# Expert results scattered to token order, context attention by halves, and slot experts with maxima found early and a split final product

## What is computed

```python
x = x + latent_attention(ctx, layernorm(x))        # 16 heads of 64; stage A
x = x + moe_top1(layernorm(x))                     # 8 experts, gelu, 1 choice; stage B
x = x + context_attention(layernorm(x), ctx)       # 16 heads of 16, 77 keys; stage C
x = x + (x_n + moe_sinkhorn(x_n))                  # 8 experts, 2 choices, gates; stage D
x = x + context_attention(layernorm(x), ctx)       # stage E
h = x_n + self_attention(rms(x_n)); x = x + h + moe_top2(rms(h))   # stage F
x = x + align(ctx, layernorm(x))                   # dynamic time warping; stage G
# stage H, slot experts: b batch, m token, n expert (64), p slot (32), d width
logits = einsum('bmd,dnp->bmnp', x_n, phi)
dispatch = softmax(logits, axis=0)                 # over the two batches
combine = softmax(logits over (n, p), axis=-1)
slots = einsum('bmd,bmnp->bnpd', x_n, dispatch)
y = einsum('bnpd,nde->bnpe', slots, W) + b
x = x + einsum('bnpd,bmnp->bmd', y, combine)
```

## Time and profile before

| | |
|---|---|
| three runs | 3989.61, 3993.71, 4001.67 us |
| profiled execution | 3996.7 us, its span 3994.9 us |
| granted clock of TensorE, mean | 0.872 |
| busy, share of the span | TensorE 75%, VectorE 53%, ScalarE 37%, GpSimd 25% |
| A, latent attention | 1200.0 us, TensorE busy 1075.7 |
| B, experts, one choice | 200.6 us, TensorE 102.6 |
| C and E, context attention with norms | 192.7 and 193.0 us, TensorE 148.9 and 151.0 |
| D, experts, sinkhorn, two choices | 424.7 us, TensorE 266.1 |
| F, self-attention, then experts, two choices | 624.0 and 415.0 us, TensorE 537.9 and 264.3 |
| G, alignment | 278.0 us, TensorE 40.0 |
| H, slot experts: first pass, second, final product | 254.3, 96.0, 116.6 us |

### The profile page before, as it was taken

The page is one execution under the profiler, slowest core; times in us unless marked ns, Lnnn a source line. Parts: engine busy times, 40 slices in busy tenths (PEclk is TensorE's granted clock), DMA queues, the critical chain, the costliest instruction groups (busy, mean ns, idle before and its releaser), DMA issues. The chain is left out here.

```text
span 3994.9 us, 40974 instructions
## 1 busy us (share of the span) xinstructions
PE 3001.8 (75%) x14054; PEld 1774.0 (44%) x14054; DVE 2109.9 (53%) x3706; ACT 1486.7 (37%) x2035; POOL 994.6 (25%) x586
## 2 busy tenths in 40 slices
PE   3999999999984568369658599999639940069879
PEld 1555555555534534259635233333339920034354
DVE  4655555555522345347536378788237737831270
ACT  3344444444442233336323245555426510022240
POOL 1346565555542202121213100000130040001100
PEclk7899999999996779579879789999769965579999
DMA  2000000000002400156300000000036420000150
GB/s 90 5 6 1 5 5 5 0 5 5 2 0 90 132 11 0 36 187 213 122 25 0 11 3 2 4 4 2 2 142 223 160 54 10 4 21 32 47 185 21
DMA packets 81429, 187.26 MB, mean 47 GB/s; under 512 B 19011, under 2 KB 55491, under 8 KB 73216
## 3 DMA queue, kind: packets, MB, share of 16 engines
q0 software_dynamic: 16464, 103.18, 7.7%
q1 hardware_dynamic: 61856, 76.11, 6.1%
q10 hardware_dynamic: 2960, 6.03, 0.4%
HBM read 145.65 MB, written 39.38 MB: 46 GB/s over the span
## 5 line engine op out<-in xcount | busy, mean ns | idle before, releaser
L602 POOL TENSOR_TENSOR A_key_sums<-A_key_sums,A_probs 128x1024 f32<-128x1024 f32 (+1 forms) x224 | 526.7, 2370 | 228.5 <-ACT A_probs L495 228.5
L495 ACT ACTIVATE A_probs<-A_banks 128x512 f32<-128x512 f32 (+1 forms) x576 | 329.0, 597 | 384.9 <-PE A_banks L415 382.7
L545 DVE TENSOR_REDUCE A_part_max<-A_banks 128x1 f32<-128x367 f32 x768 | 353.9, 530 | 157.1 <-PE A_banks L336 155.6
L1750 DVE TENSOR_REDUCE F_part_max<-F_banks 128x1 f32<-128x512 f32 x512 | 324.9, 683 | 56.8 <-PE F_banks L1603 54.0
L1696 ACT ACTIVATE F_probs<-F_banks 128x1024 f32<-128x1024 f32 x256 | 248.0, 1022 | 233.6 <-PE F_banks L1649 233.5
L364 PE MATMUL A_banks<-A_probs,A_v_tok 128*64 128x512 f32 x1152 | 278.7, 605 | 0.0
L413 PE MATMUL A_banks<-A_q_one,A_k_one 128*128 128x512 f32 (+1 forms) x576 | 255.6, 444 | 26.2 <-ACT A_probs L495 23.1
L336 PE MATMUL A_banks<-A_k_one,A_q_one 128*128 128x368 f32 x768 | 230.2, 383 | 6.8 <-ACT A_v_tok L475 6.4
L415 PE MATMUL A_banks<-A_q_two,A_k_two 128*128 128x512 f32 (+1 forms) x576 | 227.2, 394 | 0.0
L167 POOL TENSOR_SCALAR F_r<-F_r,F_ln_w 128x512 f32<-128x512 f32 x16 | 28.8, 1812 | 656.7 <-DVE F_r L132 656.7
L336 PEld LDWEIGHTS A_banks<-A_k_one,A_q_one 128*128 128x128 f32 x768 | 147.4, 192 | 94.7 <-DVE A_part_max L545 58.5
(11 more groups left out here) (537 smaller groups left out, 6262.2 us busy)
## 6 DMA issues: line engine op xcount, KB each, us to landing
H_w<-in_H_w SPq DMA_DIRECT2D x11, 1024.0 KB, 4.8
moe_in<-A_zeros ACTq DMA_DIRECT2D x1, 5888.0 KB, 17.3
D_tile_in<-moe_in SPq DMA_DIRECT2D x23, 256.0 KB, 5.3
moe_out<-D_z SPq DMA_DIRECT2D x23, 256.0 KB, 5.0
F_tile_in<-moe_in SPq DMA_DIRECT2D x23, 256.0 KB, 5.3
moe_out<-F_z SPq DMA_DIRECT2D x23, 256.0 KB, 4.8
H_phi<-in_H_w SPq DMA_DIRECT2D x5, 1024.0 KB, 4.9
B_tile_in<-moe_in SPq DMA_DIRECT2D x15, 256.0 KB, 3.0
```

Source lines behind the costliest of these rows:

```text
L495: act.activation(probs[0:kw, j, kt % RING, blk * BLK:(blk + 1) * BLK], ps[0:kw, half % 3, :], ACT.Exp, scale=1.0 / 8.0).then_inc(s["exp_re ...
L545: dve.tensor_reduce(part_max[:, i // 3, i % 3:i % 3 + 1], ps[:, MAX_BANKS[i % 3], 0:PIECE], AX.X, ALU.max).then_inc(s["piece_max"], 1)
L602: pool.tensor_tensor(key_sums[0:kw, j, :], before, probs[0:kw, j, kt % RING, :], ALU.add).then_inc(s["summed"], 1)
L1750: op = dve.tensor_reduce(part_max[:, maximum_at(hd, qt), kb:kb + 1], bank, AX.X, ALU.max)
```

## The change

The words of the change name an alignment in wave order; the alignment's code is the same in both kernels. What differs:

- **Scratch tensors.** Each expert layer has its own `moe_in` and `moe_out` in DRAM. `moe_in` has one more column (B) or five more (D, F) in each row. B's is zeroed at the start from ScalarE's queue, D's and F's from SyncE's within the latent attention.
- **Routing in the rows.** The added columns say for each row to which token it belongs, which expert was its first choice, and the gates. They take seven more small steps of VectorE before the rows are sent (one with one choice) and two more small loads.
- **Scattered results.** Per slot, VectorE works out from the loaded rows where each result goes (`find_rows`, four small steps, one with one choice) and multiplies the result by its gate where it copied it (L1093 for L1033). GpSimd scatters it with two indirect DMAs per slot to `moe_out`, which is now in token order by choice, with room behind for unused rows. In the tail SyncE loads blocks of 512 KB, TensorE adds the two choices by products with the identity, VectorE adds to x. The gathers and L1066, L1067 are gone.
- **Context attention by halves.** Maximum and difference run on two halves of 616, each with its own count; the scores of a half wait for the difference of that half only. The last block's four outputs use four banks and do not wait for each other.
- **Slot experts.** The maxima are found in the first pass, 1,024 numbers in each of the 32 steps, and one small one at its end. The second pass takes groups 12 to 15 first, whose slots are in SBUF, with the first group's weights loaded at the end of the first pass. The final product is a block of its own: its two factors are split into halves by ScalarE and VectorE, and TensorE does three single passes for each product.

The diff, cut:

```diff
-            sp.wait_ge(slots_zeroed, 16)
+            zero_rows(sp, t["scratch_F_in"], zeros, slots_zeroed)
+            sp.wait_ge(slots_zeroed, 16 * len(MOE_CHOICES))
...
             def load(i):
                 if i >= LOADS:
                     sp.wait_ge(s["turned_ps"], i - LOADS + 1)
+                    sp.wait_ge(s["dest_ready"], i - LOADS + 1)
                 sp.dma_start(tile_in[:, i % LOADS], rows_of(slots_dram, i)).then_inc(tile_loaded[i % LOADS], 16)
...
+            for g in range(NBLK):
+                if g >= GATHERS:
+                    sp.wait_ge(s["back_ps"], g - GATHERS + 1)
+                for k in range(K):
+                    at = ((g % GATHERS) * K + k) * BT
+                    sp.dma_start(taken[:, at:at + BT, :], from_tokens(g, k)).then_inc(back_loaded[g], 16)
...
+            def store(i):
+                pool.wait_ge(s["z_ready"], i + 1)
+                pool.wait_ge(s["dest_ready"], i + 1)
+                for h in range(H):
+                    pool.indirect_dma_start(out=made_dram, in_=z[:, i % ZS, h, :], in_offset=None,
+                                            out_offset=bass.IndirectOffsetOnAxis(ap=dest_of[:, i, h:h + 1], axis=0))\
+                        .then_inc(z_stored[i % ZS], 16)
...
+                if i >= RAWS:
+                    store(i - RAWS)
+            for i in range(SLOTS - RAWS, SLOTS):
+                store(i)
...
             for g in range(NBLK):
-                if K == 2:
-                    pe.wait_ge(s["gated"], BT * (g + 1))
-                else:
-                    pe.wait_ge(gathered[g], gathered_before + 16 * BT)
+                pe.wait_ge(back_loaded[g], 16 * K)
...
+                        for k in range(K):
+                            at = ((g % GATHERS) * K + k) * BT + n
+                            mm = pe.matmul(ps[:, 1 + C * (g % 2) + c, n * P:(n + 1) * P], taken[:, at, c * P:(c + 1) * P],
+                                           consts["ident"][:, :], start=k == 0, stop=k == K - 1)
                 mm.then_inc(s["back_ps"], 1)
...
+            def find_rows(i):
+
+                dve.wait_ge(tile_loaded[i % LOADS], 16 * (i // LOADS + 1))
+                rows = tile_in[:, i % LOADS]
+                if K == 1:
+                    own = rows[:, :, D]
+                else:
+                    dve.tensor_scalar(choice[:, i], rows[:, :, FIRST_EXPERT:FIRST_EXPERT + 1], group_expert[:, i:i + 1], None,
+                                      ALU.is_equal).then_inc(s["chosen"], 1)
+                    dve.wait_ge(s["chosen"], i + 1)
+                    dve.tensor_tensor(route[:, i], rows[:, :, SWAP], choice[:, i].broadcast_to([P, H, 2]),
+                                      ALU.mult).then_inc(s["swapped"], 1)
+                    dve.wait_ge(s["swapped"], i + 1)
+                    dve.tensor_tensor(route[:, i], route[:, i], rows[:, :, OTHER], ALU.add).then_inc(s["routed"], 1)
+                    dve.wait_ge(s["routed"], i + 1)
+                    own = route[:, i, :, 0]
+                dve.scalar_tensor_tensor(out=dest_of[:, i, :], in0=own, scalar=float(K * T), in1=slot_c[:, i, :],
+                                         op0=ALU.add, op1=ALU.add).then_inc(s["dest_ready"], 1)
...
             def lo(i):
+                find_rows(i)
                 dve.wait_ge(s["hi_ready"], i + 1)
...
                 else:
-                    dve.tensor_copy(z[:, i % ZS], bank).then_inc(s["z_ready"], 1)
+                    left = dve.tensor_tensor(z[:, i % ZS], bank, route[:, i, :, 1:2].broadcast_to([P, H, D]), ALU.mult)
+                left.then_inc(s["z_ready"], 1)
...
-                if g:
-                    add(g - 1)
-            add(NBLK - 1)
+                add(g)
```

```diff
-                    if n:
-                        pe.wait_ge(s["diff_ready"], n)
-                    for i in range(2 * C):
-                        mm = pe.matmul(ps[:, i, 0:HALF], q[:, i // 2, n * P:(n + 1) * P],
-                                       k_spread[:, n * P // S, i // 2, (i % 2) * HALF:(i % 2 + 1) * HALF],
-                                       start=True, stop=True)
-                    mm.then_inc(s["score_ps"], 1)
+                    for g in range(C):
+                        if n:
+                            pe.wait_ge(s["diff_ready"], C * (n - 1) + g + 1)
+                        for a in range(2):
+                            mm = pe.matmul(ps[:, 2 * g + a, 0:HALF], q[:, g, n * P:(n + 1) * P],
+                                           k_spread[:, n * P // S, g, a * HALF:(a + 1) * HALF], start=True, stop=True)
+                        mm.then_inc(s["score_ps"], 1)
...
                 def before_exp(n):
-                    dve.wait_ge(s["score_ps"], n + 1)
-                    banks = ps[:, 0:2 * C, 0:HALF].rearrange("p a (h k) -> p a h k", k=CTX)
-                    if n >= 2:
-                        dve.wait_ge(s["exp_ready"], n - 1)
-                    dve.tensor_reduce(top[:, n % 2], banks, AX.X, ALU.max).then_inc(s["top_ready"], 1)
-                    dve.wait_ge(s["top_ready"], n + 1)
-                    dve.tensor_tensor(heads_of(diff, n), banks, top[:, n % 2].unsqueeze(3).broadcast_to(by_head),
-                                      ALU.subtract).then_inc(s["diff_ready"], 1)
+                    for g in range(C):
+                        dve.wait_ge(s["score_ps"], C * n + g + 1)
+                        banks = ps[:, 2 * g:2 * g + 2, 0:HALF].rearrange("p a (h k) -> p a h k", k=CTX)
+                        dve.tensor_reduce(top[:, n % 2, 2 * g:2 * g + 2], banks, AX.X, ALU.max).then_inc(s["top_ready"], 1)
+                    for g in range(C):
+                        banks = ps[:, 2 * g:2 * g + 2, 0:HALF].rearrange("p a (h k) -> p a h k", k=CTX)
+                        if n >= 2:
+                            dve.wait_ge(s["exp_ready"], n - 1)
+                        dve.wait_ge(s["top_ready"], C * n + g + 1)
+                        dve.tensor_tensor(heads_of(diff, n)[:, 2 * g:2 * g + 2], banks,
+                                          top[:, n % 2, 2 * g:2 * g + 2].unsqueeze(3).broadcast_to(by_half),
+                                          ALU.subtract).then_inc(s["diff_ready"], 1)
```

```diff
+        middle = ExitStack()
+        mc = Scope(nc, middle, "Hm")
+        RING = 3
+        staged = mc.sb("staged", [P, B, C, BLK])
+        part_max, nmax = mc.sb("part_max", [P, B, TB, Q]), mc.sb("nmax", [P, TILES])
+        w_loaded = [mc.sem(f"w_loaded{n}") for n in range(RING)]
+        GQ = G // Q
+        order = list(range(G - GQ, G)) + list(range(G - GQ))
+
...
+        w = [as_weights(staged[:, :, :, :]), as_weights(phi[:, :, :, :])]
...
                 store(Q - 2)
                 sp.wait_ge(s["stored"], 16 * B * (Q - 1))
+                sp.dma_start(w[0], t["H_w"][order[0]]).then_inc(w_loaded[0], 16)
...
+                    dve.wait_ge(s["kept0"], n + 1)
+                    dve.wait_ge(s["kept1"], n + 1)
+                    dve.tensor_reduce(part_max[:, :, m, q], logits[:, m::TB, q * BLK:(q + 1) * BLK], AX.X, ALU.max)\
+                       .then_inc(s["maximum"], 1)
```

and, in the second pass, the groups in that order (`order`) and the product in a block of its own:

```diff
-                for g in range(G):
+                for i, g in enumerate(order):
                     if g // GQ < Q - 1 and g % GQ == 0:
                         pe.wait_ge(slots_loaded[g // GQ], 16 * B)
-                    pe.wait_ge(w_loaded[g % RING], 32 * (g // RING + 1))
-                    if g >= 2:
-                        pe.wait_ge(s["made_ready"], B * (g - 1))
...
+            parts = [(b, g, half) for b in range(B) for g in range(G) for half in range(HALVES)]
...
+            @block.scalar
+            def _(act):
+                for n, (b, g, half) in enumerate(parts):
+                    m = n // HALVES
+                    if half == 0:
+                        if n >= RING:
+                            act.wait_ge(s["used"], n - RING + HALVES)
+                        act.activation(made[:, m % (RING // 2), 0], group(b, g), ACT.Copy).then_inc(s["made_hi"], 1)
+                    if n >= RING:
+                        act.wait_ge(s["used"], n - RING + 1)
+                    act.activation(split(n, 0), part_of(b, g, half), ACT.Copy).then_inc(s["share_hi"], 1)
...
+                for n, (b, g, half) in enumerate(parts):
+                    m = n // HALVES
+                    if half == 0:
+                        dve.wait_ge(s["made_hi"], m + 1)
+                        dve.tensor_tensor(made[:, m % (RING // 2), 1], group(b, g), made[:, m % (RING // 2), 0].bitcast(F32),
+                                          ALU.subtract).then_inc(s["made_lo"], 1)
+                    dve.wait_ge(s["share_hi"], n + 1)
+                    dve.tensor_tensor(split(n, 1), part_of(b, g, half), split(n, 0).bitcast(F32), ALU.subtract)\
...
+            def _(pe):
+                for n, (b, g, half) in enumerate(parts):
+                    m = n // HALVES
+                    pe.wait_ge(s["made_lo"], m + 1)
```

(7 more changed lines are left out.)

292 lines of the change are left out of this document (162 added, 130 removed).

## The result

The changed kernel takes 3886.14 us in the median of four runs (3881.81 to 3889.99), the one before 3995.78 (3989.61 to 4001.67): a ratio of 0.9719, 95% interval 0.9707 to 0.9731. Forecast were 3912 us in a range of 3880 to 3944. The profiled execution took 3885.98 us, its span is 3883.9 us; the span before was 3994.9, so 111.0 us went where the sum had 82.

A forecast was written before the change was run, and what follows sets the result against it. Bounds: TensorE in the final product, VectorE's chain in the slot experts' second pass, GpSimd's gathers in expert tails. Terms −21 −16 +0.3 −22 −40 +6 +11 = −82 us gave 3915, or 3912 against the median; range 3880 to 3944.

The forecast's parts named there:

- the sum: Whole kernel: all predicted gains and costs of the changed stretches added together, claimed to take 82 us off the profiled execution.

## What to carry to other kernels

Read slack as the distance between the starts of two instructions, compared with that of the same pair when nothing waits, not as the idle in brackets: a small step added to an engine that looks full may be free, and the next one of the same size is not. Where a chain is shortened, look at what TensorE does just before the next stage, since the clock that it leaves is paid or earned there. And a pass that is one part waiting and one part work comes down to what the longest single engine needs, and then to its start: of the 71.9 us of the second pass 60 are TensorE's own pace, 5 the start and 7 the transfers of the first groups, and with all loads issued at once the tail is TensorE's 16.4 us behind its first load. Last, when a run without some work is the test, compare it group by group: its total can hide that it paid for something else, here the clock of its first group.

## What had not been expected of the hardware

- The same code starts a stage at either clock. In the final product TensorE idles 3.65 us first; the granted clock of the next 8 us was 1.00 in two traces, 0.79 in two and 0.57 in four, and the stage took 97.0 to 97.1, 98.5 and 99.5 to 99.9 us. In context attention the same made 3 us in E, and up to 4 in C (−10.8 to −14.9 with the same code).
- Small instructions on 2 to 4 columns in a chain by semaphores start 0.20 us apart (0.26 after the first) also in the middle of a full loop.
- Dummy transposes in a row came with holes without any semaphore between them, in stage D: four of 1.0 to 1.7 us in one row of 32, two of 1.1 and 0.45 us in the row of 96, while a row of 64 ran without one. What makes them was not tried.
